# Gram lower triangle on one core: TensorE's loop entered at its last half tile, row turns moved behind the odd tile, one store moved behind the last load

## The chip, the core and the metric

The kernel runs on one core of one Trainium2 chip. The metric is the device time of one execution in microseconds. Everything is float32. TensorE multiplies, VectorE transposes 32x32 blocks, ScalarE copies out of the matmul banks and packs, GpSimd packs what crosses partitions, and SyncE (SP) issues the loads.

## The reference

For each of 2048 batches there is a matrix X of 64 rows and 256 columns. Z = X Xᵀ is 64 x 64, and the output is its strictly lower triangle, row by row, 2016 numbers per batch.

```
Z = jnp.einsum('bnd,bmd->bnm', inputs, inputs)
li, lj = jnp.tril_indices(64, k=-1)
return Z[:, li, lj]
```

134.2 MB are read and 16.5 MB written.

## The kernel before

**Tiles.** A tile is 16 batches, 1 MB of input; there are 128 tiles. SP loads tile t into slot t % 11 of the ring x_in (L193 to L202); from tile 11 on each load waits until tile t-11 has been turned. VectorE turns a tile into x_turned (turn, L242), so that the inner dimension lies on partitions. TensorE multiplies it (multiply, L313): 8 chunks of the inner dimension x 2 slots x 4 quadrants x 2 sides, 128 matmuls in the program, which the profile records as 256 matmuls and 256 weight loads. ScalarE copies the bank set into products (keep, L350).

**The lap.** TensorE's code is a loop over laps of two tiles. The even tile (j = 0) is turned in one transpose of 128x2048 and multiplied behind one wait; the odd tile (j = 1) is turned in two transposes of 128x1024 (chunks 0 to 3 and 4 to 7) and multiplied in two halves, each with its own wait and semaphore. Near the end of each tile TensorE also waits until the other bank set has been copied out. To have one code for all laps, the loop is entered at its second tile (the body "second", L343), so a blank tile of zeros comes first: VectorE and GpSimd fill x_turned[:, 1] with zeros (L278, L222). Its product is never copied out. In memory the code of the body "lap" stands first, then "second".

**Groups.** Eight tiles are a group of 128 batches; there are 16 groups, 0 to 15. When all eight are copied out, VectorE turns the group's rows in 4 pieces of 16 rows (turn_rows, L256), into row_halves; each is one transpose of 128x1024. PIECE_LAG = 10 sets when: behind the turn of tile t, for t = 10, 12, 14 and so on, so behind an even tile, one piece per lap. At t = 126 the remaining pieces of group 14 follow together. ScalarE packs the triangle out of row_halves into packed_rows (pack, L366), in quarters of a piece, two after each tile; GpSimd carries the parts that change partitions (L226 to L232). packed_rows has two buffers, for even and odd groups; before a buffer is written again, ScalarE and GpSimd wait until the stores out of it have landed (wait_packed_free, L149). Group 15 is turned into last_halves, which lies in slots 0 and 1 of x_in, by turn_last_rows (L272).

**Stores.** Groups below LATE_STORES = 13 are stored from ScalarE's queue, after a tile's copy (L393 to L400): even groups in two DMAs of 504 KB, odd groups up to 11 in one of 504, one of 252 and four of 63 KB, spread over the following tiles. The groups from LATE_STORES to 14 are stored by SP behind all its loads (L204 to L207), group 14's other side by ScalarE (L411), and group 15 in three parts by both.

Of the kernel before, what the change touches and what calls it, by code (L numbers as in the profile page):

```python
# [8 lines left out]
HALF = PARTS // 2  # L9
# [10 lines left out]
def gram_lower_triangle(nc: bass.Bass, x: bass.AP, y: bass.AP):  # L20
# [34 lines left out]

    PIECE_LAG = GROUP_TILES + 2
    PACK_LAG = 2 * PIECE_LAG - 2


    BY_POOL = (11, 16)
# [2 lines left out]
                  slice(0, first_column(BLOCK))]  # L65


    FEW, FEW_UNTIL = 4, GROUPS - 4

    LATE_STORES = GROUPS - 3  # L70
    WHOLE_SIDES = [(side, 0, BLOCK) for side in range(SIDES)]
    FIRST_LANES = [(0, 0, BLOCK), (1, 0, BLOCK // 2)]
    FEW_LANES = [(1, q, q + FEW) for q in range(BLOCK // 2, BLOCK, FEW)]
# [4 lines left out]
    with ExitStack() as stack:  # L78
# [3 lines left out]
        def semaphore(name):  # L82
# [14 lines left out]

        last_halves = x_in[:, 0:ROWS * KEPT // (JOINED * DIM)].rearrange(
            "p k (i h j) -> p (k i) h j", h=RUNS, j=BLOCK)

        loaded = [semaphore(f"loaded{k}") for k in range(IN_RING)]

# [41 lines left out]
        def stores_before(group):  # L144

            return sum(16 * len(FIRST_LANES + FEW_LANES if by_few(g) else WHOLE_SIDES)
                       for g in range(group % 2, min(group, GROUPS - 1), 2))

        def wait_packed_free(engine, group):  # L149

            if group >= 2:
                engine.wait_ge(stored[group % 2], stores_before(group))

        def halves(group):
            return last_halves if group == GROUPS - 1 else row_halves

        def pack_short(copy, group, i):
            at = first_column(i)
            return copy(packed_rows[:, group % 2, :, at:at + i], halves(group)[:, i, :, 0:i])  # L159

        def pack_long_pair(copy, group, i):

            at = first_column(i)
            two = packed_rows[:, group % 2, :, at:at + 2 * i].rearrange("p h (w c) -> p h w c", w=2)
            return copy(two[:, :, :, 0:BLOCK], halves(group)[:, i:i + 2].rearrange("p w h j -> p h w j"))  # L165

        def carry_across(copy, group, i, side):

            first, at = side * HALF, first_column(i)
            return copy(packed_rows[first:first + BLOCK, group % 2, :, at + BLOCK:at + i],  # L170
                        halves(group)[first + BLOCK:first + HALF, i, :, 0:i - BLOCK])

        def store(engine, group, columns, lanes):

            rows = y[group * GROUP:(group + 1) * GROUP, columns].rearrange("(h q s) c -> s q h c", h=RUNS, s=SIDES)
            for side, first, end in lanes:
                engine.dma_start(rows[side, first:end],  # L177
                                 packed_rows[side * HALF + first:side * HALF + end, group % 2, :, columns]).then_inc(
                    stored[group % 2], 16)

        def store_last(engine, side, part):
# [58 lines left out]
        @block.vector  # L240
        def _(dve):
            def turn(t):  # L242

                k, (lap, j) = t % IN_RING, place(t)
                dve.wait_ge(loaded[k], (t // IN_RING + 1) * 16)
                for h in range(PARTIALS[j]):
                    chunks = slice(chunks_of(j, h).start, chunks_of(j, h).stop)
                    if laps_done(j, lap) > 0:
                        dve.wait_ge(multiplied[j][h], laps_done(j, lap))  # L249
                    nc.vector.transpose(  # L250
                        x_turned[:, j, chunks].rearrange(
                            "p c b s (h u n v) -> p u v (c b s h) n", h=ROWS // BLOCK, u=PAIRS, v=PAIR),
                        x_in[:, k].rearrange("p (r d) -> p r d", r=JOINED)[
                            :, :, chunks.start * BLOCK:chunks.stop * BLOCK]).then_inc(turned[j][h], LAP)

            def turn_rows(n):  # L256
                group, piece = divmod(n, PIECES)
                rows = piece_rows(piece)
                if piece == 0:

                    wait_kept(dve, (group + 1) * GROUP_TILES - 1)
                if group > 0:

                    dve.wait_ge(packed_home, n - PIECES + 1)
                    if piece < LONG_PIECES:
                        dve.wait_ge(packed_across, (group - 1) * LONG_PIECES + piece + 1)  # L266
                nc.vector.transpose(  # L267
                    row_halves[:, rows].rearrange("p i h (n u v) -> p (i h) u n v", u=PAIRS, v=PAIR),
                    products[:, group % KEPT_RING, rows, :].rearrange("p i (h q) -> p (i h) q", q=BLOCK)).then_inc(
                    rows_turned, 1)  # L270

            def turn_last_rows(run, rows):  # L272

                return nc.vector.transpose(  # L274
                    last_halves[:, rows, run].rearrange("p i (n u v) -> p i u n v", u=PAIRS, v=PAIR),
                    products[:, (GROUPS - 1) % KEPT_RING, rows, run * BLOCK:(run + 1) * BLOCK])

            nc.vector.memset(x_turned[:, 1, 0:CHUNKS // 2], 0.0).then_inc(turned[1][0], LAP)  # L278
            turned_rows = 0
            for t in range(TILES):  # L280
                turn(t)
                if t >= PIECE_LAG and (t - PIECE_LAG) % 2 == 0:
                    turn_rows(turned_rows)
                    turned_rows += 1
                if t == TILES - 2:

                    for n in range(turned_rows, (GROUPS - 1) * PIECES):
                        turn_rows(n)

            for run in range(RUNS - 1):  # L290
                wait_kept(dve, (GROUPS - 1) * GROUP_TILES + (run + 1) * GROUP_TILES // RUNS - 1)
                turn_last_rows(run, slice(0, ROWS))
            wait_last_kept(dve, True)
            turn_last_rows(RUNS - 1, slice(BLOCK, ROWS)).then_inc(rows_turned, LONG_PIECES)
            wait_last_kept(dve, False)
            turn_last_rows(RUNS - 1, slice(0, BLOCK)).then_inc(rows_turned, PIECES - LONG_PIECES)
            wait_packed_free(dve, GROUPS - 1)
            dve.wait_ge(rows_turned, GROUPS * PIECES)  # L298
            for piece in range(LONG_PIECES):
                rows = piece_rows(piece)  # L300
                for i in range(max(BLOCK + 1, rows.start), rows.stop):
                    last = carry_across(nc.vector.tensor_copy, GROUPS - 1, i, 1)
                last.then_inc(last_carried, 1)
            for i in range(1, BY_POOL[0]):
                last = pack_short(nc.vector.tensor_copy, GROUPS - 1, i)
            last.then_inc(last_packed, 1)

        @block.tensor
        def _(pe):

            count = nc.alloc_register(pe.engine, "count")

            def multiply(j):  # L313

                for h in range(PARTIALS[j]):
                    pe.wait_ge(turned[j][h], count)
                    for slot in range(SLOTS):
                        last_slot = h == PARTIALS[j] - 1 and slot == SLOTS - 1
                        if j == LAP - 1 and last_slot:
                            pe.reg_add(count, count, LAP)  # L320
                        for c in chunks_of(j, h):
                            if last_slot and c == CHUNKS - 2:

                                pe.wait_ge(kept[1 - j], count)
                            for g in range(QUADRANTS):
                                for side in range(SIDES):
                                    rows = x_turned[g * BLOCK:(g + 1) * BLOCK, j, c, slot, side]


                                    done = nc.tensor.matmul(  # L330
                                        bank_sets[j][side * HALF:(side + 1) * HALF, g, slot, :].rearrange(
                                            "r (n u v) -> r u n v", u=PAIRS, v=PAIR),
                                        rows,
                                        rows.rearrange("d (h u e) -> d u h e", h=ROWS // BLOCK, u=PAIRS),
                                        start=c == 0 and slot == 0, stop=c == CHUNKS - 1 and slot == SLOTS - 1)

                    done.then_inc(multiplied[j][h], 1)

            pe.reg_mov(count, LAP)
            pe.br("second")  # L340
            with nc.body("lap", valid_engines=[pe.engine]):
                multiply(0)
            with nc.body("second", valid_engines=[pe.engine]):  # L343
                multiply(1)
                pe.br_lt(count, (LAPS + 1) * LAP, on_true="lap", on_false="laps_done")
            nc.switch_bb("laps_done")

# [90 lines left out]
```

## Time and profile before

| | |
|---|---|
| median of 3 runs | 391.2 us (391.16 to 391.91) |
| profiled execution | 390.45 us |
| its span, first to last instruction | 388.6 us |
| TensorE matmul, weight load | 363.6, 358.6 us busy, 33024 records each |
| VectorE | 364.5 us busy, 297 instructions |
| ScalarE | 191.1 us busy, 867 instructions |
| GpSimd | 198.6 us busy, 971 instructions |
| DMA | 150.98 MB, mean 389 GB/s |

The span covers the instructions; the execution's own time has 1.85 us more around it. Busy times do not add up to the span, because the engines work side by side. Matmuls are pipelined, so a busy TensorE is not one at its peak, and one of its instructions may last longer in the profile than the distance to the next. Names in the profile: PE is TensorE, PEld its weight loads, DVE VectorE, ACT ScalarE, POOL GpSimd, SP SyncE; a q behind a name is the engine's sequencer.

### The profile page before, as it was taken

What the parts mean: (1) busy time and instruction counts of PE and PEld (TensorE: products, weight loads), DVE (VectorE), ACT (ScalarE), POOL (GpSimd) and SP (SyncE); (2) the same over time, 40 slices, a digit from 0 to 9 for tenths busy, and PEclk for the clock granted to TensorE, in tenths of its full rate; (3) what the DMA queues carried; (4) which work ended last, traced back from release to release, by engine and by line L of the source; (5) the groups of instructions that cost most, each with busy time, mean ns of one, the idle gap of its engine ahead of it and who ended that gap; (6) DMA issues with size and microseconds to landing.
All of it is one profiled execution on the core that took longest, in us unless ns stands there. A gap on an engine that the chain in (4) does not pass through costs nothing.

```text
span 388.6 us, 68930 instructions
## 1 busy us (share of the span) xinstructions
PE 363.6 (94%) x33024; PEld 358.6 (92%) x33024; DVE 364.5 (94%) x297; ACT 191.1 (49%) x867; POOL 198.6 (51%) x971
## 2 busy tenths in 40 slices
PE   1499999999999999999999999999999999999970
PEld 1499999999999999999999999999999999999970
DVE  3267899999999999999999999999999999999996
ACT  0032246464545555555555555545564545555565
POOL 1000083664828375482827557382846638283766
PEclk9999999999999999999999999999999999999995
DMA  8999999999999999999999999999999999993525
GB/s 309 425 419 422 424 422 417 422 420 423 421 422 420 423 422 421 423 419 422 419 424 418 422 414 425 407 421 422 421 421 370 426 423 422 423 413 141 191 56 164
DMA packets 21433, 150.98 MB, mean 389 GB/s; under 512 B 2720, under 2 KB 2848, under 8 KB 5024
## 3 DMA queue, kind: packets, MB, share of 16 engines
q1 hardware_dynamic: 18912, 136.29, 85.5%
q10 hardware_dynamic: 2496, 14.45, 9.1%
q14 instruction: 21, 0.17, 0.1%
q8 instruction: 4, 0.07, 0.1%
HBM read 134.22 MB, written 16.52 MB: 388 GB/s over the span
## 4 chain that ended last, share of the span: by engine, by line
PE 80%; DMA 7%; DVE 6%; issue 5%; ACT 1%; ACTq 0%; DVEq 0%
PE bank_set L330 80%; DMA x_in<-x_dram 7%; DVE x_turned L250 4%; DVE row_halves L267 1%; DVE packed_rows L170 1%; ACT packed_rows L159 1%; DVE x_in L274 0%; DVE x_turned L278 0%; ACTq L177 0%; ACT products L360 0%; DVEq L249 0%; DVEq L266 0%; ACTq L187 0%; DVEq L298 0%; DVEq L136 0%
## 5 line engine op out<-in xcount | busy, mean ns | idle before, releaser
L330 PE MATMUL bank_set<-x_turned 32*64 32x64 f32 x33024 | 363.6, 235 | 13.6 <-issue 13.3
L330 PEld LDWEIGHTS bank_set<-x_turned 32*64 32x64 f32 x33024 | 358.6, 131 | 18.5 <-issue 13.7
L250 DVE STREAM_TRANSPOSE x_turned<-x_in 128x1024 f32<-128x1024 f32 (+1 forms) x192 | 291.3, 1568 | 19.1 <-PE bank_set L330 13.9
L170 POOL COPY packed_rows<-row_halves 32x32 f32<-32x32 f32 (+30 forms) x930 | 191.6, 206 | 182.7 <-DVE row_halves L267 145.1
L360 ACT COPY products<-bank_set 128x512 f32<-128x512 f32 x129 | 75.1, 583 | 155.0 <-PE bank_set L330 137.0
L267 DVE STREAM_TRANSPOSE row_halves<-products 128x1024 f32<-128x1024 f32 x60 | 72.2, 1205 | 0.0
L159 ACT COPY packed_rows<-row_halves 128x32 f32<-128x32 f32 (+30 forms) x465 | 61.2, 217 | 6.5 <-DVE row_halves L267 6.5
L165 ACT COPY packed_rows<-row_halves 128x128 f32<-128x128 f32 x240 | 54.1, 299 | 9.2 <-DVE row_halves L267 8.8
L360 ACT ACT_TABLE_LOAD x1 | 1.3, 1283 | 21.6 <-PE bank_set L330 21.6
L170 POOL COPY packed_rows<-x_in 32x32 f32<-32x32 f32 (+30 forms) x31 | 5.0, 211 | 2.9 <-DVE x_in L274 2.9
L274 DVE STREAM_TRANSPOSE x_in<-products 128x1024 f32<-128x1024 f32 (+1 forms) x3 | 4.6, 1573 | 0.2 <-ACT products L360 0.2
L165 ACT COPY packed_rows<-x_in 128x128 f32<-128x128 f32 x16 | 3.3, 298 | 1.2 <-DVE x_in L274 1.2
L170 DVE COPY packed_rows<-x_in 32x32 f32<-32x32 f32 (+30 forms) x31 | 3.8, 199 | 0.1
L159 ACT COPY packed_rows<-x_in 128x62 f32<-128x62 f32 (+15 forms) x16 | 2.2, 227 | 0.8 <-DVE packed_rows L170 0.8
L278 DVE MEMSET x_turned<- 128x1024 f32 x1 | 0.9, 912 | 1.0 <-PEq L432 1.0
L222 POOL MEMSET x_turned<- 128x1024 f32 x1 | 1.0, 952 | 0.5 <-POOLq L432 0.5
L159 DVE COPY packed_rows<-x_in 128x2 f32<-128x2 f32 (+9 forms) x10 | 0.9, 171 | 0.0
L159 POOL COPY packed_rows<-x_in 128x22 f32<-128x22 f32 (+4 forms) x5 | 0.9, 222 | 0.1
L432 POOL MEMSET const-float32-0.0<- 128x1 f32 x1 | 0.1, 99 | 0.2 <-issue 0.2
L432 POOL MEMSET const-bfloat16-1.0<- 128x1 bf16 x1 | 0.1, 103 | 0.0
L432 POOL MEMSET const-uint8-127<- 128x1 uint8 x1 | 0.1, 103 | 0.0
L432 POOL MEMSET const-float32-1.0<- 128x1 f32 x1 | 0.1, 99 | 0.0
## 6 DMA issues: line engine op xcount, KB each, us to landing
x_in<-x_dram SPq DMA_DIRECT2D x128, 1024.0 KB, 18.0
y_dram<-packed_rows ACTq DMA_DIRECT2D x21, 504.0 KB, 8.0
y_dram<-packed_rows ACTq DMA_DIRECT2D x6, 252.0 KB
y_dram<-packed_rows ACTq DMA_DIRECT2D x24, 63.0 KB
y_dram<-packed_rows SPq DMA_DIRECT2D x3, 504.0 KB, 4.3
y_dram<-packed_rows SPq DMA_DIRECT2D x1, 222.0 KB
y_dram<-packed_rows ACTq DMA_DIRECT2D x1, 222.0 KB
y_dram<-packed_rows SPq DMA_DIRECT2D x1, 158.0 KB
```

Source lines behind the costliest of these rows:

```text
L159: return copy(packed_rows[:, group % 2, :, at:at + i], halves(group)[:, i, :, 0:i])
L165: return copy(two[:, :, :, 0:BLOCK], halves(group)[:, i:i + 2].rearrange("p w h j -> p h w j"))
L170: return copy(packed_rows[first:first + BLOCK, group % 2, :, at + BLOCK:at + i], halves(group)[first + BLOCK:first + HALF, i, :, 0:i - BLOCK])
L222: nc.gpsimd.memset(x_turned[:, 1, CHUNKS // 2:CHUNKS], 0.0).then_inc(turned[1][1], LAP)
L250: nc.vector.transpose(x_turned[:, j, chunks].rearrange("p c b s (h u n v) -> p u v (c b s h) n", h=ROWS // BLOCK, u=PAIRS, v=PAIR), x_in[: ...
L267: nc.vector.transpose(row_halves[:, rows].rearrange("p i h (n u v) -> p (i h) u n v", u=PAIRS, v=PAIR), products[:, group % KEPT_RING, row ...
L274: return nc.vector.transpose(last_halves[:, rows, run].rearrange("p i (n u v) -> p i u n v", u=PAIRS, v=PAIR), products[:, (GROUPS - 1) % ...
L278: nc.vector.memset(x_turned[:, 1, 0:CHUNKS // 2], 0.0).then_inc(turned[1][0], LAP)
L330: done = nc.tensor.matmul(bank_sets[j][side * HALF:(side + 1) * HALF, g, slot, :].rearrange("r (n u v) -> r u n v", u=PAIRS, v=PAIR), rows ...
L360: nc.scalar.copy(products[:, group % KEPT_RING, rows, in_group * PER_SIDE:(in_group + 1) * PER_SIDE].rearrange("p i (g b) -> p i g b", b=S ...
L432: nc = bacc.Bacc("TRN2", target_bir_lowering=False, num_devices=1)
```

## The change

There are three edits. First, TensorE's loop has three entry places: the body "lap" holds the even tile and the first half of the odd one, the body "last_half" the second half. Before the loop TensorE runs one chunk, 8 matmuls of zeros with start set, which opens the banks of set 1, signals multiplied[1][0], and jumps to "last_half". The zero fill by VectorE covers that chunk's slot alone (128 elements per partition); GpSimd's fill for the second half stays. Second, PIECE_LAG is 9: row pieces are turned behind the odd tiles t = 9, 11 and so on up to 125, and one piece remains for t = 126; PACK_LAG keeps its value, 18. Third, LATE_STORES is 12, so group 12 goes out from SP's queue behind the last load; groups 14 and 15 are packed into late_packed, two buffers in slots 7 to 10 of x_in, and no longer wait for the stores of groups 12 and 13. FEW_UNTIL goes from 12 to 11, which changes no odd group.

```
-    PIECE_LAG = GROUP_TILES + 2
-    PACK_LAG = 2 * PIECE_LAG - 2
+    PIECE_LAG = GROUP_TILES + 1
+    PACK_LAG = 2 * PIECE_LAG
...
-    FEW, FEW_UNTIL = 4, GROUPS - 4
-    LATE_STORES = GROUPS - 3
+    FEW, FEW_UNTIL = 4, GROUPS - 5
+    LATE_STORES = GROUPS - 4
...
+        late_packed = [x_in[:, k:k + 2].rearrange("p k f -> p (k f)")[:, 0:RUNS * PACKED].rearrange(
+            "p (h c) -> p h c", h=RUNS) for k in (TILES % IN_RING, TILES % IN_RING + 2)]
...
+        def packed(group):
+            return packed_rows[:, group % 2] if group < GROUPS - 2 else late_packed[group - (GROUPS - 2)]
...
-            if group >= 2:
+            if 2 <= group < GROUPS - 2:
                 engine.wait_ge(stored[group % 2], stores_before(group))
...
-            nc.vector.memset(x_turned[:, 1, 0:CHUNKS // 2], 0.0).then_inc(turned[1][0], LAP)
+            nc.vector.memset(x_turned[:, 1, 0, 0], 0.0).then_inc(turned[1][0], LAP)
...
-                if t >= PIECE_LAG and (t - PIECE_LAG) % 2 == 0:
+                if PIECE_LAG <= t < TILES - 1 and (t - PIECE_LAG) % 2 == 0:
...
-            def multiply(j):
-                for h in range(PARTIALS[j]):
-                    pe.wait_ge(turned[j][h], count)
+            def multiply_chunk(j, c, slot):
+                for g in range(QUADRANTS):
+                    for side in range(SIDES):
+                        rows = x_turned[g * BLOCK:(g + 1) * BLOCK, j, c, slot, side]
+                        done = nc.tensor.matmul(
...
+                return done
+            def multiply(j, h):
+                pe.wait_ge(turned[j][h], count)
...
             pe.reg_mov(count, LAP)
-            pe.br("second")
+            pe.wait_ge(turned[1][0], LAP)
+            multiply_chunk(1, 0, 0).then_inc(multiplied[1][0], 1)
+            pe.br("last_half")
             with nc.body("lap", valid_engines=[pe.engine]):
-                multiply(0)
-            with nc.body("second", valid_engines=[pe.engine]):
-                multiply(1)
+                multiply(0, 0)
+                multiply(1, 0)
+            with nc.body("last_half", valid_engines=[pe.engine]):
+                multiply(1, 1)
                 pe.br_lt(count, (LAPS + 1) * LAP, on_true="lap", on_false="laps_done")
```

## Rows read from the trace of the kernel before

**Rows 1.** The page: engines' busy time, and GB/s in 40 slices.

```profile
PE 363.6 (94%) x33024; PEld 358.6 (92%) x33024; DVE 364.5 (94%) x297; ACT 191.1 (49%) x867; POOL 198.6 (51%) x971
...
GB/s 309 425 419 422 424 422 417 422 420 423 421 422 420 423 422 421 423 419 422 419 424 418 422 414 425 407 421 422 421 421 370 426 423 422 423 413 141 191 56 164
```

**Rows 2.** The chain in order of time: start us, us, what.

```profile
17.29 302.10 PE bank_set L330 x16507
```

**Rows 3.** Timeline, VectorE near the start: start us, us, what, [idle before].

```profile
32.90 4.57 DVE L250 STREAM_TRANSPOSE x_turned<-x_in 128x2048 f32<-128x2048 f32 x3 [1.03 <-PE bank_set L330]
```

**Rows 4.** Timeline, VectorE from 342 to 350 us.

```profile
342.77 1.21 DVE L267 STREAM_TRANSPOSE row_halves<-products 128x1024 f32<-128x1024 f32 x1
...
343.90 4.54 DVE L250 STREAM_TRANSPOSE x_turned<-x_in 128x1024 f32<-128x1024 f32 x3
...
348.37 1.20 DVE L267 STREAM_TRANSPOSE row_halves<-products 128x1024 f32<-128x1024 f32 x1
```

**Rows 5.** Loads issued in 60:100, then in 250:300 us.

```profile
DMA to landing us min/median/max: 10.7/12.3/13.6
...
DMA to landing us min/median/max: 21.2/23.9/27.3
```

**Rows 6.** Loads of tiles 111, 119 and 127: issue, and to landing.

```profile
L199 SPq DMA_DIRECT2D x_in<-x_dram x1: 328/328/328, 298.1 to 298.1; - x1
...
DMA to landing us min/median/max: 27.3/27.3/27.3
...
L199 SPq DMA_DIRECT2D x_in<-x_dram x1: 327/327/327, 320.5 to 320.5; - x1
...
DMA to landing us min/median/max: 28.8/28.8/28.8
...
L199 SPq DMA_DIRECT2D x_in<-x_dram x1: 328/328/328, 342.9 to 342.9; - x1
```

**Rows 7.** Timeline: row turn and tile 111's turn; tile 119's turn.

```profile
325.99 1.20 DVE L267 STREAM_TRANSPOSE row_halves<-products 128x1024 f32<-128x1024 f32 x1
327.12 1.20 DVE L250 STREAM_TRANSPOSE x_turned<-x_in 128x1024 f32<-128x1024 f32 x1
...
349.49 4.67 DVE L250 STREAM_TRANSPOSE x_turned<-x_in 128x1024 f32<-128x1024 f32 x3
```

**Rows 8.** Timeline of the first 22 us.

```profile
5.04 1.75 PE L330 MATMUL bank_set<-x_turned 32*64 32x64 f32 x94 [5.04 <-issue]
7.08 2.31 DVE L250 STREAM_TRANSPOSE x_turned<-x_in 128x2048 f32<-128x2048 f32 x1 [5.14 <-DMA x_in<-x_dram]
10.71 2.25 PE L330 MATMUL bank_set<-x_turned 32*64 32x64 f32 x128 [3.92 <-issue]
...
18.30 1.25 DVE L250 STREAM_TRANSPOSE x_turned<-x_in 128x1024 f32<-128x1024 f32 x1 [5.40 <-PE bank_set L330]
21.64 1.28 ACT L360 ACT_TABLE_LOAD   x1 [21.64 <-PE bank_set L330]
```

**Rows 9.** DMA queue q8 in 0:20, then whole: packets, MB, share.

```profile
q8 instruction: 3, 0.05, 1.0%
...
q8 instruction: 4, 0.07, 0.1%
```

**Rows 10.** Timeline of the end.

```profile
370.80 2.33 DVE L267 STREAM_TRANSPOSE row_halves<-products 128x1024 f32<-128x1024 f32 x2
...
374.31 2.95 PE L330 MATMUL bank_set<-x_turned 32*64 32x64 f32 x256 [0.34 <-DVE x_turned L250]
...
376.35 0.37 ACTq L177 DMA_DIRECT2D y_dram<-packed_rows  x1
```

**Rows 11.** Group 12's store (issue, to landing); SP's stores from group 13 on.

```profile
L177 ACTq DMA_DIRECT2D y_dram<-packed_rows x2: 327/390/452, 337.7 to 338.0; - x2
...
DMA to landing us min/median/max: 7.2/8.8/10.3
...
358.77 26.98 SPq L177 DMA_DIRECT2D y_dram<-packed_rows  x6
```

More of the change, by code:

```diff
@@ L158, in pack_short @@
             at = first_column(i)
-            return copy(packed_rows[:, group % 2, :, at:at + i], halves(group)[:, i, :, 0:i])
+            return copy(packed(group)[:, :, at:at + i], halves(group)[:, i, :, 0:i])
         def pack_long_pair(copy, group, i):
             at = first_column(i)
-            two = packed_rows[:, group % 2, :, at:at + 2 * i].rearrange("p h (w c) -> p h w c", w=2)
+            two = packed(group)[:, :, at:at + 2 * i].rearrange("p h (w c) -> p h w c", w=2)
             return copy(two[:, :, :, 0:BLOCK], halves(group)[:, i:i + 2].rearrange("p w h j -> p h w j"))
@@ L169, in carry_across @@
             first, at = side * HALF, first_column(i)
-            return copy(packed_rows[first:first + BLOCK, group % 2, :, at + BLOCK:at + i],
+            return copy(packed(group)[first:first + BLOCK, :, at + BLOCK:at + i],
                         halves(group)[first + BLOCK:first + HALF, i, :, 0:i - BLOCK])
@@ L177, in store @@
                 engine.dma_start(rows[side, first:end],
-                                 packed_rows[side * HALF + first:side * HALF + end, group % 2, :, columns]).then_inc(
+                                 packed(group)[side * HALF + first:side * HALF + end, :, columns]).then_inc(
                     stored[group % 2], 16)
@@ L311, in _ @@
             count = nc.alloc_register(pe.engine, "count")
-            def multiply(j):
-                for h in range(PARTIALS[j]):
-                    pe.wait_ge(turned[j][h], count)
[L317 to L337, printed above, removed]
@@ new lines, in multiply_chunk @@
+            def multiply_chunk(j, c, slot):
[3 more added lines that the diff above has]
+                        done = nc.tensor.matmul(
+                            bank_sets[j][side * HALF:(side + 1) * HALF, g, slot, :].rearrange(
+                                "r (n u v) -> r u n v", u=PAIRS, v=PAIR),
+                            rows,
+                            rows.rearrange("d (h u e) -> d u h e", h=ROWS // BLOCK, u=PAIRS),
+                            start=c == 0 and slot == 0, stop=c == CHUNKS - 1 and slot == SLOTS - 1)
+                return done
@@ new lines, in multiply @@
+            def multiply(j, h):
+                pe.wait_ge(turned[j][h], count)
+                for slot in range(SLOTS):
+                    last_slot = h == PARTIALS[j] - 1 and slot == SLOTS - 1
+                    if j == LAP - 1 and last_slot:
+                        pe.reg_add(count, count, LAP)
+                    for c in chunks_of(j, h):
+                        if last_slot and c == CHUNKS - 2:
+                            pe.wait_ge(kept[1 - j], count)
+                        done = multiply_chunk(j, c, slot)
+                done.then_inc(multiplied[j][h], 1)
```

## The prediction

> **What bounds the kernel now.** I read the page's busy shares first, then the chain of waits, the timelines of start and end, and the landing times of loads. TensorE and VectorE are each busy for 94% and DMA moves some 421 GB/s up to the last five slices [rows 1], so the page alone does not say which of them a saving must reach. The chain has one unbroken TensorE piece from 17.29 to 319.39 us [rows 2]. There are three regimes.
>
> The lap of two tiles: with no finished rows to turn, VectorE is busy for 4.57 us and waits 1.03 for TensorE [rows 3]: TensorE's lap is 5.60. Later VectorE's lap is a row turn at 342.77, two half turns and a full one from 343.90, and the next row turn at 348.37: also 5.60, with no idle time [rows 4]. Both are full; neither can catch up.
>
> The loads: tile t's load goes out when tile t-11 is turned, some 30 us ahead of its use. It takes a median 12.3 us to land in 60:100 and 23.9 in 250:300 [rows 5]: DMA is full, and every store pushes the loads later. Near the end the margin is nearly gone. Tile 111 lands at 298.1 + 27.3 = 325.4 and is turned at 327.12: 1.7 early. Tile 119: 320.5 + 28.8 = 349.3 against 349.49: 0.2 [rows 6, 7]. A TensorE further ahead than these margins waits for loads.
>
> The entry: TensorE starts at 5.04, idles 3.92 before 10.71, and 4.33 before 17.29 [rows 2, 8], in "issue", so for no semaphore.
>
> **Entering at the last half.** Before, a whole blank tile runs: 94 + 128 matmul records, then 34 behind 17.29 (256 a tile, two per matmul of the program, each with a weight load). The instruction queue q8 fetches three times in 0:20 and once later, 0.07 MB in four [rows 9], 16 KB a time. Between two stops stand 128 matmuls with 128 weight loads, 256 instructions. So I read a stop as the first visit to a block of 256 instructions, at 3.9 to 4.3 us.
>
> The new layout follows. The body "second" began with 94 pairs (189 instructions) left in the third block, at about 578; some 514 of those ahead are tile 0's code, 64 the preamble. The chunk of 8 matmuls adds 16 pairs, 32 instructions. The body "last_half" then starts at about 867: 78 of its 128 pairs lie in block four, 50 in block five. Block three is first reached inside tile 0, after some 208 of its 256 pairs. Three stops again, one now in real work.
>
> Step by step: the chunk takes 16 x 19 ns (1.75 / 94, [rows 8]) = 0.3, and I put 0.3 for its wait for the zero fill (estimate), so the last half starts 0.6 later, at 5.6. 78 x 19 ns = 1.5: 7.1. A stop, 4.1: 11.2. 50 pairs, 0.9: 12.1. Tile 0 is turned by 7.08 + 2.31 = 9.4, and took from 18.2 (VectorE was released at 18.30) to 21.64, 3.4 us [rows 8]; 208 of 256 pairs are 2.8: 14.9. A stop, 4.3: 19.2. The rest 0.6: 19.8. Lead 1.8 us. Bounds: if block three comes ahead of need, 12.1 + 3.4 = 15.5, a lead of 6.1; if one more stop is paid, 1.8 - 4.3 = -2.5. I take 1.8, because in the trace every new block is waited for.
>
> The Trainium skill (Runtime: NRT & Kernel Launch, section Instruction fetch mechanics) says that instructions come in 16 KiB blocks of 256, prefetched sequentially, and that a taken branch out of a two-page window forces a fetch. Its block size agrees with the 128 pairs between the stops. Its two-page window would stop every lap at the jump back; the trace disagrees: unbroken from 17.29 on. Its hidden sequential prefetch would make the lead 6.1; the stops of 3.92 and 4.33 speak against that.
>
> **Row turns behind the odd tile.** The count stays 60; only VectorE's order changes: from full, row turn, half, half to full, half, half, row turn. A lap's sum stays 5.60, and the rows it needs were copied off the banks a tile earlier. The price: an odd tile is turned where the row turn stood, 1.13 us sooner (343.90 - 342.77, [rows 4]), and its load must land that much sooner. Tile 111's margin falls from 1.7 to 0.6 (325.99 against 325.4), tile 119's from 0.2 to -0.9 [rows 6, 7]. Alone, this edit loses the 0.9 and gains the 0.5 below: +0.4. ScalarE and GpSimd get the rows sooner; both have idle time, 49% and 51% busy [rows 1], so that is worth nothing.
>
> At the end it gains. Before, VectorE turned two row pieces between tiles 126 and 127 (370.80, 2.33 us), so TensorE waited 0.34 for tile 127 at 374.31 and took 2.95 for it, to 377.26 [rows 10]. Now one of the two stands ahead of tile 126, and VectorE is ready 1.1 sooner. TensorE flows from 373.97 at half a lap per tile, 2.80: 376.77, a gain of 0.5. ScalarE must be free to copy: its half store at 376.35 takes 0.37 [rows 10], just in time, and what it packs before that comes sooner as well. Each us that it is late would come off this gain. Bounds 0 to 0.5; I take 0.5.
>
> **Group 12's store behind the last load.** Its two issues leave ScalarE's queue at 337.7 [rows 11] for SP's, behind tile 127's load at 342.9 [rows 6]. 2 x 504 KB are 1.03 MB, at 421 GB/s 2.45 us of all DMA engines. Loads from tile 118 or 119 on land up to 2.45 sooner: tile 119 at 346.9, wanted at 348.37. Margin 1.5 there, where it would have been -0.9. Bounds: 0 if the late DMA engines are late for another reason, 2.45 as taken. The tail pays nothing: the last load lands by 342.9 + 28.8 - 2.45 = 369.3, group 12's store behind it by 371.7, group 13's (issued at 358.77, [rows 11]) by 374.2, ahead of group 14's halves at 376.35, and DMA moves only 56 to 191 GB/s from about 350 on [rows 1]. ScalarE's two issues (0.33 to 0.45 each, [rows 11]) fall into idle time.
>
> The late buffers in x_in take away waits that would bite now: group 14's last piece is turned at 370.80 [rows 10], its first three laps sooner, at 354; held for a store that lands at 371.7, ScalarE would be over 10 us late. With the buffers nobody waits for it.
>
> The Trainium skill (DMA: Bandwidth & Descriptors, section Queues, rings and completion order) says that a queue's descriptors are consumed in ring order on each DMA engine, while the engine takes turns between queues. The trace agrees: ScalarE's store landed after 7.2 to 10.3 us, a load took 28.8 [rows 6, 11]. By that rule a store in SP's own queue cannot delay a load.
>
> **The sum**, against the profiled execution (390.45 us: span 388.6 and 1.85 around it). The lead of 1.8 lasts until the loads bind. The tightest place is then tile 111: 0.6, less 0.1 from landing to start, leaves 0.5 from there on. With the end's 0.5 that is 1.0: 389.45. The median of the runs, 391.2, lies 0.75 above the profiled execution; if that is lateness of loads, it moves the old bound (tile 119) and the new one (tile 111) alike, so I take the same 1.0 off: 390.2 us.
>
> **Rivals.**
> 1. The loads do not bind at tile 111: the whole 1.8 is kept, 1.8 + 0.5 = 2.3: 388.9. For: the margin is a small difference of large numbers, and 1.3 us earlier landing is enough. Against: the loads fall behind steadily [rows 5].
> 2. Nothing to measure. Either the end's gain alone is left (tile 111 lands 0.5 later, or the entry is not earlier at all, since a stop stays in tile 0): 390.7. Or the store's move relieves the wrong DMA engines and the odd tiles' earlier turns meet late loads: 391.6. For: tile 119's margin of 0.2. Against: 2.45 us of traffic fewer in exactly that stretch.
> 3. Slower: the entry skips three blocks where it skipped one, and one more of them is missing at the jump back into the loop. Tile 0 then ends 2.5 us later than before; TensorE is unbroken behind it, so 2.5 - 0.5 = +2.0: 393.2. It decides if four stops of 4 us stand ahead of tile 0's end; my count is three. Against: before, the first two blocks were there at that jump, without a stop.
>
> **How the numbers follow.** Forecast 0.50 (own range 389.6 to 390.4), rival 1 0.12, rival 2 0.28, rival 3 0.10. The measurement can tell 0.2%, 0.8 us, from no change. Faster 0.62, within it 0.28, slower 0.10. Range 388.7 to 391.8: all but rival 3.
>
> **What would show it.** TensorE: 16 matmul records before 2.5 us, three stops, one of them inside tile 0, whose end is at 19 to 20 us. A lead of 1.8 us at 100 us, of 0.5 at 340. VectorE idle for a load at tile 111 or near it. The last tile's matmuls directly behind tile 126's. Time to landing under 27 us from tile 119 on. It is wrong if tile 0 ends after 21.6, if loads bind at tiles 119 to 121 again, or if the end is more than the 11.3 us of before (388.6 - 377.26) behind the last matmul.

## The result: 14.5 us slower, and the loss stands in the first 45 us

The changed kernel takes 405.55 us (405.2 to 406.27, 6 runs), the kernel before 391.01 in the same comparison: ratio 1.0374, 95% interval 1.0358 to 1.039. I had forecast 390.2. In the profiled execution the span is 403.8 us against 388.6, 15.2 more.

The page of the kernel after answers to [rows 1]: TensorE is as busy in us as before, but in a longer span, and the loss is at its left end.

```profile
PE 366.2 (91%) x32912; PEld 360.8 (89%) x32912; DVE 364.4 (90%) x297; ACT 186.1 (46%) x867; POOL 197.1 (49%) x971
...
PE   2425999999999999999999999999999999999980
...
PEclk9955999999999999999999999999999999999996
...
GB/s 323 423 418 302 287 373 371 362 358 426 419 422 400 403 427 416 419 393 426 422 420 409 411 425 419 419 377 425 412 425 393 421 422 422 424 369 219 157 26 179
```

Four slices pass before TensorE is full (before, two). DMA falls to 287 GB/s in the fifth, because the load ring is full and is emptied late (the loads of tiles 13 and 14 go out at 28.3 and 39.5): the loads are ahead now. The timeline of the kernel after answers to [rows 8]. Its columns: start us, us, what, and in brackets the idle time ahead.

```profile
1.05 0.52 PE L329 MATMUL bank_set<-x_turned 32*64 32x64 f32 x16 [1.05 <-DVE x_turned L287]
...
6.45 1.54 PE L329 MATMUL bank_set<-x_turned 32*64 32x64 f32 x78 [4.88 <-issue]
...
13.12 4.41 PE L329 MATMUL bank_set<-x_turned 32*64 32x64 f32 x256 [5.12 <-issue]
...
24.76 2.26 PE L329 MATMUL bank_set<-x_turned 32*64 32x64 f32 x128 [7.24 <-issue]
25.93 1.28 ACT L377 ACT_TABLE_LOAD   x1 [25.93 <-PE bank_set L329]
...
30.96 2.26 PE L329 MATMUL bank_set<-x_turned 32*64 32x64 f32 x128 [3.94 <-issue]
...
36.99 23.25 PE L329 MATMUL bank_set<-x_turned 32*64 32x64 f32 x1987 [3.77 <-issue]
...
44.71 0.58 ACT L377 COPY products<-bank_set 128x512 f32<-128x512 f32 x1 [2.14 <-PE bank_set L329]
```

The counts of pairs (a weight load and its matmul) come first: 16, 78, then 256, which is the blank half's last 50 pairs and tile 0's first 206. Up to there it is the forecast. Then a stop of 7.24 and, 128 pairs apart, two more that I had not foreseen. ScalarE's first instruction is released by the end of tile 0's product, at 25.93 (before, 21.64). The last row is the copy of tile 3; before it stood at 29.97. The delay there, 14.74 us, is nearly that of the whole run, since every engine runs in step behind it: the copy of tile 125 is 15.6 us late, that of tile 127 15.06.

DMA queue q8, which fetches code, answers to [rows 9]: 0:20, 20:50, and the whole run.

```profile
q8 instruction: 3, 0.05, 0.9%
...
q8 instruction: 4, 0.07, 0.9%
...
q8 instruction: 7, 0.11, 0.1%
```

Seven fetches where there were four. The trace has each fetch as one packet of q8, of 16 KB, so the DMA view in narrow windows places them. Times are us from the span's start.

| packet of q8 | TensorE, changed kernel |
|---|---|
| 4.00 to 4.88 | resumes at 6.45, block four |
| 10.65 to 11.63 | resumes at 13.12, block five |
| 16.80 to 17.83 | no stop ends; block three is reached at 17.53 |
| 22.39 to 23.46 | resumes at 24.76, block three |
| 28.51 to 29.61 | resumes at 30.96, block four |
| 34.51 to 35.61 | resumes at 36.99, block five |
| 38.13 to 39.08 | no stop ends |

In all runs of this document TensorE resumes 1.2 to 1.6 us behind the end of a packet, at every stop in "issue" (in the kernel before the packets end at 3.63, 9.24 and 15.91, and TensorE resumes at 5.04, 10.71 and 17.29). So the stops are waits for code. Which block a packet holds the trace does not say; the table gives the block that TensorE enters.

The wait of the first jump itself is a row too, of TensorE's sequencer: 4072 ns before (first fence), 5272 after (second).

```profile
L340 PEldq COMPARE_BRANCH  x1: 4072/4072/4072, 0.9 to 0.9; - x1
```

```profile
L356 PEldq COMPARE_BRANCH  x1: 5272/5272/5272, 1.1 to 1.1; - x1
```

Loads of tiles 111 and 119 (answer to [rows 6], and their turns to [rows 7]): 313.6 + 20.7 = 334.3, turned at 341.53, 7.2 us early; 336.0 + 22.2 = 358.2, turned at 363.95, 5.7 early. Nothing waits for a load late in this run.

```profile
L207 SPq DMA_DIRECT2D x_in<-x_dram x1: 328/328/328, 313.6 to 313.6; - x1
...
DMA to landing us min/median/max: 20.7/20.7/20.7
...
L207 SPq DMA_DIRECT2D x_in<-x_dram x1: 328/328/328, 336.0 to 336.0; - x1
...
DMA to landing us min/median/max: 22.2/22.2/22.2
...
341.53 1.20 DVE L258 STREAM_TRANSPOSE x_turned<-x_in 128x1024 f32<-128x1024 f32 x1
...
363.95 1.20 DVE L258 STREAM_TRANSPOSE x_turned<-x_in 128x1024 f32<-128x1024 f32 x1
```

The end answers to [rows 10]: one row turn ahead of tile 127 in place of two, and TensorE has no wait for VectorE in its last piece; ScalarE's half store ends 0.1 us ahead of the last copy (before, 0.6).

```profile
386.37 1.21 DVE L275 STREAM_TRANSPOSE row_halves<-products 128x1024 f32<-128x1024 f32 x1
387.50 2.33 DVE L258 STREAM_TRANSPOSE x_turned<-x_in 128x1024 f32<-128x1024 f32 x2
...
391.89 0.38 ACTq L185 DMA_DIRECT2D y_dram<-x_in  x1
392.36 0.65 ACT L377 COPY products<-bank_set 128x256 f32<-128x256 f32 x2 [0.50 <-PE bank_set L329]
```

### The profile page after: what moved, and what is told of

It reads as the page before. It is cut to its first block, busy times and chain, and to the rows that moved or that the text cites. A ratio compares the mean times of both kernels' runs of the same rounds, so it can differ in the third digit from the quotient of the medians.

```text
span 403.8 us, 68701 instructions
## 1 busy us (share of the span) xinstructions
PE 366.2 (91%) x32912; PEld 360.8 (89%) x32912; DVE 364.4 (90%) x297; ACT 186.1 (46%) x867; POOL 197.1 (49%) x971
## 4 chain that ended last, share of the span: by engine, by line
DVE 39%; PE 36%; issue 23%; ACT 1%; POOL 0%; DVEq 0%; ACTq 0%; POOLq 0%
PE bank_set L329 36%; DVE x_turned L258 29%; DVE row_halves L275 10%; DVE x_in L178 1%; ACT x_in L167 1%; DVE x_in L282 0%; POOL x_turned L230 0%; DVEq L274 0%; ACTq L185 0%; ACT products L377 0%; DVEq L257 0%; ACTq L195 0%; POOLq L227 0%; DVEq L140 0%; POOLq L229 0%
## 5 line engine op out<-in xcount | busy, mean ns | idle before, releaser
L178 POOL COPY packed_rows<-row_halves 32x32 f32<-32x32 f32 (+30 forms) x868 | 177.4, 204 | 186.5 <-DVE row_halves L275 151.4
L167 ACT COPY packed_rows<-row_halves 128x32 f32<-128x32 f32 (+30 forms) x434 | 57.2, 219 | 0.0
L173 ACT COPY packed_rows<-row_halves 128x128 f32<-128x128 f32 x224 | 50.5, 301 | 4.9 <-issue 4.9
L178 POOL COPY x_in<-row_halves 32x32 f32<-32x32 f32 (+30 forms) x62 | 12.7, 204 | 9.7 <-DVE row_halves L275 7.2
L178 POOL COPY x_in<-x_in 32x32 f32<-32x32 f32 (+30 forms) x31 | 4.9, 210 | 5.9 <-DVE x_in L282 5.9
L167 ACT COPY x_in<-row_halves 128x32 f32<-128x32 f32 (+30 forms) x31 | 3.9, 218 | 0.0
L173 ACT COPY x_in<-x_in 128x128 f32<-128x128 f32 x16 | 3.3, 295 | 1.1 <-DVE x_in L282 1.1
L178 DVE COPY x_in<-x_in 32x32 f32<-32x32 f32 (+30 forms) x31 | 3.7, 199 | 0.0
L173 ACT COPY x_in<-row_halves 128x128 f32<-128x128 f32 x16 | 3.6, 303 | 0.0
```

The source lines that it names most:

```text
L167: return copy(packed(group)[:, :, at:at + i], halves(group)[:, i, :, 0:i])
L178: return copy(packed(group)[first:first + BLOCK, :, at + BLOCK:at + i], halves(group)[first + BLOCK:first + HALF, i, :, 0:i - BLOCK])
```

## The experiments

**Which edit it is.** The kernel before with the new entry alone:

```
-            pe.br("second")
+            pe.wait_ge(turned[1][0], LAP)
+            multiply_chunk(1, 0, 0).then_inc(multiplied[1][0], 1)
+            pe.br("last_half")
```

> The kernel before with the new entry alone (chunk, jump to last_half, small zero fill). Theory J (jump over blocks of code): the jump skips block three, so that block and then the two behind it are fetched again inside tiles 0 and 1: five stops as in the changed kernel, 7 fetches on q8, tile 3 copied 14.7 us later than before, and since nothing catches up, the whole time is 14.5 to 15.5 us over before (405.5 to 406.5). Rival R (the row turn order or the moved store costs the time): within 1 us of before, 390 to 392.

Measured: 406.38 us, ratio 1.0396 (1.0372 to 1.0419), 7 fetches, and the same sequence on TensorE with a first long stop of 8.74:

```profile
12.91 4.00 PE L320 MATMUL bank_set<-x_turned 32*64 32x64 f32 x256 [4.58 <-issue]
25.66 2.25 PE L320 MATMUL bank_set<-x_turned 32*64 32x64 f32 x128 [8.74 <-issue]
31.86 2.25 PE L320 MATMUL bank_set<-x_turned 32*64 32x64 f32 x128 [3.95 <-issue]
37.90 7.33 PE L320 MATMUL bank_set<-x_turned 32*64 32x64 f32 x508 [3.79 <-issue]
```

The entry is the whole loss. Tile 3 is copied 15.9 us later than before, where I had expected 14.7; the first jump (5612 ns) and the long stop are longer than in the changed kernel. Its complement, the changed kernel with the old entry:

```
-            multiply_chunk(1, 0, 0).then_inc(multiplied[1][0], 1)
-            pe.br("last_half")
+            pe.br("second")
```

> The changed kernel with the old entry (jump to the second body, whole blank tile), so row turns behind the odd tile and group 12 behind the last load alone. Theory J: 0.5 us less at the last tile, as the changed kernel's trace shows (15.6 us late at tile 125, 15.06 at tile 127), and up to 0.9 us more from a lap that is 0.01 us longer: ratio 0.998 to 1.001, 390.2 to 391.4. Rival R: 400 to 406.

Measured: 390.29 against 391.01, ratio 0.9981 (0.9971 to 0.9991): 0.7 us faster. The other two edits one by one, first PIECE_LAG = GROUP_TILES + 1 alone:

> The kernel before with PIECE_LAG 9 alone: row turns behind the odd tile. By my forecast's terms: 0.5 us gained at the last tile, 0.9 lost where tile 119's load lands late: +0.4, 391.4; VectorE idle for a load near 349 us. If the longer lap of the changed kernel (0.01 us, 64 laps) comes from this order, up to 0.7 more. If loads do not bind: -0.5, 390.5.

Measured: 390.58 us, ratio 0.9996 (0.9984 to 1.0007), no change to be seen. In its trace tile 119's load lands 0.7 us ahead of its turn and no turn behind tile 0's waits for a load, so the forecast loss of 0.9 did not come; the copies drift 0.6 us later against the kernel before between tiles 3 and 118 (a lap of 5.60 in place of 5.59), and the last two tiles win 0.55 back. Then the store and the late buffers alone (FEW_UNTIL goes along):

```
-    LATE_STORES = GROUPS - 3
+    LATE_STORES = GROUPS - 4
```

> The kernel before with the store of group 12 behind the last load and the late buffers alone. By my forecast's terms tile 119's load lands 2.45 us sooner relative to its turn, and TensorE gains only the 0.1 us that it lost there: 390.8 to 391.1. If the loads of before bind more than its profiled execution shows (the median is 0.75 over it), up to 0.8 less: 390.2.

Measured: 390.42 us, ratio 0.9986 (0.9975 to 0.9996), 0.6 us faster. In its profile the smallest margin of a load behind tile 1 is 2.4 us (tile 114), where it was 0.1 (tile 120). That more is gained than the 0.1 us of the profiled execution would fit loads that bind in the kernel's common run, which is 0.75 us longer than the profiled one; no profile of such a run exists, so this is not shown.

**Is it the skipped block?** First the chunk with a jump to the first block not yet fetched, block three, where the odd tile's first half lies. The chunk is closed by itself (alone sets its stop) and signals nothing; the zero fill is the large one again.

```
-            multiply_chunk(1, 0, 0).then_inc(multiplied[1][0], 1)
-            pe.br("last_half")
+            multiply_chunk(1, 0, 0, alone=True)
+            pe.br("odd")
             with nc.body("lap", valid_engines=[pe.engine]):
                 multiply(0, 0)
+            with nc.body("odd", valid_engines=[pe.engine]):
                 multiply(1, 0)
-            with nc.body("last_half", valid_engines=[pe.engine]):
                 multiply(1, 1)
```

> The changed kernel with its chunk of 8 matmuls (opened and closed by itself), but the jump behind it goes to the first half of the odd tile, so to the next block of code (block three), and the whole blank odd tile runs. Theory J (the jump over a block is the cause): three stops as in the kernel before, at 79, 128 and 49 pairs (32 instructions of chunk shift the borders by 16 pairs), 4 fetches on q8, tile 3 some 1 to 2.5 us later than before for the later first jump, 391.5 to 393.5. Rival K (the chunk or the split of the loop's code costs it, wherever the jump goes): 404 to 407.

Measured: 394.49 us, 1.0088 (1.0064 to 1.0112). Three stops, ahead of 78, of 128 and of the rest, and 4 fetches:

```profile
1.99 0.52 PE L329 MATMUL bank_set<-x_turned 32*64 32x64 f32 x16 [1.99 <-DVE x_turned L287]
9.16 1.55 PE L329 MATMUL bank_set<-x_turned 32*64 32x64 f32 x78 [6.65 <-issue]
14.72 2.25 PE L329 MATMUL bank_set<-x_turned 32*64 32x64 f32 x128 [4.02 <-issue]
21.32 30.91 PE L329 MATMUL bank_set<-x_turned 32*64 32x64 f32 x2707 [4.35 <-issue]
```

So the chunk and the split bodies are innocent. The time is 1 us over my range: the jump stands behind the fill and the chunk and waits 7032 ns (resumed at 9.16, before at 5.04). Second, five more chunks ahead of the jump, to move every border:

```
+            for _ in range(5):
+                multiply_chunk(1, 0, 0, alone=True)
             multiply_chunk(1, 0, 0).then_inc(multiplied[1][0], 1)
```

> The changed kernel with six chunks ahead of the jump in place of one, 160 instructions more, so last_half begins at about 1027, the start of block five. Theory J: all borders move by 80 pairs: one stop at the entry, 128 pairs of the blank half and 128 of tile 0 without a stop, then a long stop (7 to 9 us) for block three, and block four and five fetched after it with a stop of 3.8 to 4 each, 128 pairs apart; one fetch fewer on q8 (6), and some 4 us less than the changed kernel: 401 to 402.5. If the stops go with the jump and not with blocks of 256 instructions, the pairs between them stay 78, 256, 128, 128 and the time 405 to 408.

Measured: 407.80 us, 1.0427 (1.0391 to 1.0463), 7 fetches where I had expected 6. I had missed a border by two pairs:

```profile
1.05 1.78 PE L329 MATMUL bank_set<-x_turned 32*64 32x64 f32 x96 [1.05 <-DVE x_turned L287]
8.98 2.25 PE L329 MATMUL bank_set<-x_turned 32*64 32x64 f32 x126 [6.15 <-issue]
14.35 2.66 PE L329 MATMUL bank_set<-x_turned 32*64 32x64 f32 x128 [3.12 <-issue]
21.37 2.26 PE L329 MATMUL bank_set<-x_turned 32*64 32x64 f32 x128 [4.36 <-issue]
27.85 2.26 PE L329 MATMUL bank_set<-x_turned 32*64 32x64 f32 x128 [4.22 <-issue]
34.05 2.25 PE L329 MATMUL bank_set<-x_turned 32*64 32x64 f32 x128 [3.94 <-issue]
39.52 12.70 PE L329 MATMUL bank_set<-x_turned 32*64 32x64 f32 x974 [3.22 <-issue]
```

The blank half no longer fits block five: 126 pairs, a stop, 2 pairs in block six; then 126 pairs of tile 0, and blocks three to six one after another, 128 pairs each. The borders moved with the instructions, as blocks of 256 must; six blocks are in play, so the time rose where I forecast a fall. The time alone would fit the rival (405 to 408); the counts of pairs do not.

The very long stop is gone here, 4.36. The packets of q8 fit a fetch of block six that stood in the way in the changed kernel. There the packet from 16.80 to 17.83 ends no stop, TensorE reaches block three at 17.53, and the next packet ends 5.6 us behind it: 7.24 is the rest of one fetch, a whole one, and the 1.3 us up to the next matmul. Here TensorE leaves block six after 2 pairs, and no packet lies between the one that ends at 13.04, for block six, and the one that ends at 19.87, behind which block three starts.

Third, the same entry with an empty stub in block three that holds only a jump:

> The changed kernel, entered at the same last half in the same place in memory, but by way of block three: the jump behind the chunk goes to a stub between tile 0's code and the odd tile's first half (at about 612, block three), which holds only a jump to last_half (block four); tile 0's code jumps over the stub in each lap. Theory J (skipping block three is the cause): block three is there when tile 0 needs it, so blocks four and five are not fetched again: 4 or 5 fetches on q8 in place of 7, 256 pairs of tile 0 in one piece, tile 3 copied 9 to 13 us sooner than in the changed kernel, 392 to 396. Rival K2 (entering with block four as the first fetched one, or jumping back from it over two blocks, is the cause): 7 fetches, 404 to 407.

Measured: 406.16 us, 1.0388, 7 fetches. It tested nothing: the stub held no other instruction, and the program laid out has no jump of its line, nor one over it. So the opening chunk itself was put into block three:

```
-            multiply_chunk(1, 0, 0).then_inc(multiplied[1][0], 1)
-            pe.br("last_half")
+            pe.br("opening")
             with nc.body("lap", valid_engines=[pe.engine]):
                 multiply(0, 0)
+                pe.br("first_half")
+            with nc.body("opening", valid_engines=[pe.engine]):
+                multiply_chunk(1, 0, 0).then_inc(multiplied[1][0], 1)
+                pe.br("last_half")
+            with nc.body("first_half", valid_engines=[pe.engine]):
                 multiply(1, 0)
```

> The changed kernel with the opening chunk itself placed in block three, between tile 0's code and the odd tile's first half, followed by the jump to last_half in block four. The entry jumps to the chunk; tile 0's code jumps over it in each lap (k_stub's stub held no instruction and was laid out away, so it tested nothing). Theory J (block three was skipped, so the blocks behind it were fetched twice): the first jump waits 4.1 us as in the kernel before, then 16 pairs, 78, 50; tile 0 runs in one piece; 4 fetches on q8; tile 3 copied within 1 us of the kernel before's 29.97, whole time 390 to 392.5. Rival K2 (the last half as entry, whatever was visited ahead of it, is the cause): 7 fetches and 404 to 407.

Measured: 399.58 us, 1.0226 (1.0207 to 1.0246). The start is nearly as forecast: four fetches and tile 0 in one piece behind the third stop. The first jump waits 4964 ns, not 4.1 us, and tile 3 is copied at 31.37, so 1.4 us later than before (I had said within 1) and 13.3 sooner than in the changed kernel.

```profile
6.06 0.52 PE L329 MATMUL bank_set<-x_turned 32*64 32x64 f32 x16 [6.06 <-issue]
11.93 1.53 PE L329 MATMUL bank_set<-x_turned 32*64 32x64 f32 x77 [5.35 <-issue]
17.56 32.67 PE L329 MATMUL bank_set<-x_turned 32*64 32x64 f32 x2758 [4.10 <-issue]
...
80.13 0.58 ACT L381 COPY products<-bank_set 128x512 f32<-128x512 f32 x1 [1.51 <-PE bank_set L329]
...
194.76 0.59 ACT L381 COPY products<-bank_set 128x512 f32<-128x512 f32 x1 [1.51 <-PE bank_set L329]
...
L358 PEldq COMPARE_BRANCH  x64: 163/163/176, 22.2 to 383.6; - x64
```

Same entry point, block three visited ahead of it, and no block is fetched twice: the skip is the cause. But the whole time is 7 us over my range. The copies of tiles 20 and 60 are 114.63 us apart, 5.73 a lap: the jump over the opening takes 163 ns each time, and here nearly all of it is paid: 0.14 us.

**An order with no skip.** The last half placed first in memory, right behind the chunk; the lap then has a jump more.

```
+            with nc.body("last_half", valid_engines=[pe.engine]):
+                multiply(1, 1)
+                pe.br_lt(count, (LAPS + 1) * LAP, on_true="lap", on_false="laps_done")
             with nc.body("lap", valid_engines=[pe.engine]):
                 multiply(0, 0)
                 multiply(1, 0)
-            with nc.body("last_half", valid_engines=[pe.engine]):
-                multiply(1, 1)
-                pe.br_lt(count, (LAPS + 1) * LAP, on_true="lap", on_false="laps_done")
+                pe.br("last_half")
```

> The changed kernel with last_half placed first in memory, right behind the chunk, and an unconditional jump at the end of the lap's first part: nothing is skipped at the entry, but each lap has a second jump. Theory J: no block is fetched twice, 4 fetches on q8 or fewer; the blank half runs at once; blocks three, four and five are met in tiles 0 and 1 at 79, 128 and 128 pairs. If each is fetched only when it is reached, three stops of 4 us in real work, tile 1 ends near 28.6 (before 24.3). If the next block is fetched while TensorE waits for tile 0's load, one or two stops are gone and tile 1 ends at 20 to 25. The second jump costs 0 to 0.1 us in each of 64 laps. Together 390 to 401. Rival K (entering at the last half is bad wherever it lies): 404 or more.

Measured: 389.93 against 391.16, ratio 0.9963 (0.9948 to 0.9978), at the very low end of my 390 to 401.

```profile
1.97 2.26 PE L329 MATMUL bank_set<-x_turned 32*64 32x64 f32 x128 [0.40 <-POOL x_turned L230]
...
7.97 3.49 PE L329 MATMUL bank_set<-x_turned 32*64 32x64 f32 x206 [3.73 <-DVE x_turned L258]
...
15.27 2.27 PE L329 MATMUL bank_set<-x_turned 32*64 32x64 f32 x128 [3.81 <-issue]
...
21.47 30.78 PE L329 MATMUL bank_set<-x_turned 32*64 32x64 f32 x2683 [3.93 <-issue]
```

Entering at the last half is not bad in itself. Tile 0 crosses into block three after some 79 pairs, within the 206 of that row, without a stop: q8's first packet ends at 7.65, while TensorE waited 3.73 us for tile 0. Blocks four and five begin 6.2 us apart (15.27, 21.47), of which 2.3 are work. The extra jump costs nothing that the lap shows here: of the lap's two jumps one takes 76 ns and one 169, together 245, where the one before took 208; and the lap is 5.59.

**What sets the 6 us?** f_last_half_first with fewer loads outstanding at the start:

```
             def load(t):
                 k = t % IN_RING
+                if 2 <= t < 8:
+                    sync.wait_ge(loaded[(t - 2) % IN_RING], 16)
```

> f_last_half_first, and SP issues the loads of tiles 2 to 7 only when the load two tiles ahead of each has landed, so no more than two loads are outstanding up to some 20 us. Theory Q (a block of code costs 6.2 us from one to the next, because its fetch of 16 KB queues behind outstanding loads): the fetches follow each other in 4 to 5 us, the stops of 3.8 and 3.9 fall to 1.5 to 2.5, tile 1 is copied at 20 to 22 us in place of 24.67. Of this lead the loads let 1.5 us through (the smallest margin of f_last_half_first, 1.58 us at tile 111), so 388 to 389. Rival F (the time of a fetch is fixed): the same stops, and the same time as f_last_half_first, 389.9, or later if the loads fall behind.

Measured: 390.80 us, ratio 0.9994 (0.9979 to 1.0008); I had expected 388 to 389 if outstanding loads delay the fetches, and 389.9 or later if they do not. The first stop fell to 1.16 us, the second did not, and tile 1 was copied at 21.68, 3 us sooner. Then loads bound: two of VectorE's four waits for loads are those of tiles 0 and 1, the others those of tiles 103 and 111; tiles 103, 111 and 113 were turned the moment they had landed, and the lead was all but gone by tile 110.

```profile
12.51 1.62 PE L331 MATMUL bank_set<-x_turned 32*64 32x64 f32 x128 [1.16 <-issue]
18.43 13.77 PE L331 MATMUL bank_set<-x_turned 32*64 32x64 f32 x1074 [4.31 <-issue]
...
DVE x_turned L260 <- DMA x_in<-x_dram: 8.0, 4, 4.6
```

With three outstanding (3 <= t < 8, waiting for t - 3):

> The same with three loads outstanding. Theory Q: between f_last_half_first and g_f_pace2 at the stops (2.5 to 3.5 us), and DMA never idle, 388.3 to 389.5. Rival F: 389.9.

Measured: 389.39 against 391.22, ratio 0.9949 (0.9935 to 0.9963), the fastest of all here, 1.8 us under the kernel before and 16.2 under the changed one. Its stops are 3.35 and 3.94, and tile 1 is copied 0.24 us sooner than in f_last_half_first; the 0.5 us between these two kernels' times is not clear of noise, since their intervals overlap. The pacing of two on the kernel before:

> The kernel before with the same pacing as g_f_pace2 alone. Theory Q: stops of 1.5 to 2.5 us in place of 3.92 and 4.33, tile 1 copied 3 to 4 us sooner; but tile 119's margin of 0.2 us is used up at once, so the whole time gains 0 to 0.3 us: 390.7 to 391.2. Rival F: as before, or later by what the loads lose.

Measured: 393.61 us, 1.0057 (1.0039 to 1.0076), 2.4 us slower, where I had expected a gain of up to 0.3. Its stops are 3.10 and 4.06 and its start is 0.5 us earlier, but DMA moved 365 GB/s in 10:20, and with no margin behind it the run loses 3.5 us of that lead between tiles 100 and 120. Outstanding loads explain a part of some stops, not the 6 us. Where the fetches follow each other, the packets of q8 end 5.5 to 6.8 us apart with ten loads outstanding and with three. With two they are 3.6, 5.9 and 5.1 apart in g_f_pace2, 4.8 and 6.2 in j_before_pace2. What else makes the 6 us stays open.

Last, both ideas: i_f_pace3 with the opening chunk in block three, in the middle of tile 0's code, so one jump more in each lap than there, two more than in the kernel before.

> i_f_pace3 (last half first in memory, three loads outstanding at the start) with the opening chunk in block three, in the middle of tile 0's code, and the entry by way of it. Entering a block starts the fetch of the next, 6 us each, whatever runs there: block three is there at 5.0 (the wait of the first jump as in the kernel before, 4.1), four near 11, five near 17, in place of 9, 15 and 21. Blank half and tile 0 run on resident code from 5.4 to 11; one stop of about 4 us ahead of block five; tile 1 copied at 20 to 21 us, 3.5 us sooner than i_f_pace3. The loads let 2.3 us of it through (its smallest margin, 2.36): 387 to 388. Rival: entering block three starts nothing while the code jumps back, and block four is fetched only when it is reached: 389.4 as i_f_pace3.

Measured: 394.32 us, 1.0093 (1.0079 to 1.0106), 6.3 us over my range.

```profile
6.00 2.62 PE L331 MATMUL bank_set<-x_turned 32*64 32x64 f32 x144 [6.00 <-issue]
9.49 5.06 PE L331 MATMUL bank_set<-x_turned 32*64 32x64 f32 x332 [0.87 <-DVE x_turned L260]
18.38 31.84 PE L331 MATMUL bank_set<-x_turned 32*64 32x64 f32 x2696 [3.83 <-issue]
...
76.41 0.59 ACT L387 COPY products<-bank_set 128x512 f32<-128x512 f32 x1 [1.48 <-PE bank_set L331]
...
190.35 0.59 ACT L387 COPY products<-bank_set 128x512 f32<-128x512 f32 x1 [1.49 <-PE bank_set L331]
```

The start does nearly what was forecast: 16 pairs in block three, back for the blank half, and then 332 pairs across two borders with one stop behind them; tile 1 is copied at 21.63, 2.8 us sooner than in i_f_pace3 (forecast: 3.5). The packet behind the visit to block three ends at 10.46, and TensorE then runs through block four without a stop: the visit of 16 pairs had started the fetch of the next block, though TensorE left at once. That is not so at every visit: in h_after_pad160 the packet behind the 2 pairs in block six is block three's. But the lap is 5.70 (113.94 us for 20), and 0.1 us in each of 64 laps eats the start twice over.

## Why the prediction was wrong

**Entry: the failed step.** "Three stops again, one now in real work" was right for the three that it named (after 16, 94 and 350 pairs) and wrong in what stands behind: I took a block once fetched to stay. The runs show that after a jump over an unfetched block, that block and every block behind it are fetched when the code comes back to it in sequence (7 packets where there were 4): a stop of 7.24 us in place of the forecast 4.3 ahead of block three, and two more, of 3.94 and 3.77, ahead of blocks four and five. Tile 0 ends at 25.93, past the 21.6 that I had named as the sign of being wrong. The sum: the unbroken run starts at 36.99 in place of 17.29, 19.7 later. By then TensorE has done 462 pairs of real work (606 less 144 blank), and before it still owed 34 blank ones; these 496 pairs are 5.4 us at 5.60 / 512 ns each. 19.7 - 5.4 = 14.3, against 14.74 at tile 3; the last 0.4 I cannot place. Rival 3 came nearest: a skip of blocks that makes one of them missing at the jump back, one stop more ahead of tile 0's end, +2.0. Its mechanism was there, its size was not: as many stops stand ahead of tile 0's end as forecast, the last 2.9 us longer, and two more stand in tile 1. Its chance of 0.10 was too small for a step of which the trace of before could show nothing, since that kernel never skips.

The rule of the Trainium skill that I weighed here comes out mixed. The page Runtime: NRT & Kernel Launch (section Instruction fetch mechanics) says that the next block is prefetched in sequence and that a taken branch breaks this. I had held the stops of 3.92 and 4.33 against the first half; f_last_half_first and m_f_open_in_block3 show the prefetch, at some 6 us a block. It is hidden only where TensorE comes to the next block that much later, because it waits or runs other code meanwhile. The second half is in line with what the changed kernel paid for, though the page does not speak of fetching blocks again. Its two-page window stays refuted: no lap stops at its jump back.

**The first jump.** Forecast to resume at 5.6, it did at 6.45: the jump waits 5272 ns in place of 4072, not only 0.2 us later. The later it is issued, the longer it waited in nearly all runs here: issued at 0.9, it took 4.1 to 4.4 us; at 1.0, 4.9 to 5.0; at 1.1, 5.3 to 6.1; at 2.1, 7.0; at 2.4, 6.6.

**Row turns.** The order cost no wait for a load: in the trace of c_order_only tile 119's landed 0.7 us early where I had put it 0.9 late. A lap longer by 0.01 us, which I had put at zero, took 0.6; why it is longer stays open. The end's gain, forecast 0.5, was 0.55 in c_order_only; in the changed kernel the copies are 15.62 us late at tile 125 and 15.06 at tile 127, 0.56.

**Store.** In d_store_only tile 119's load landed 4.5 us ahead of its turn, where it was 0.2: more than the 2.45 that I had put, of which 0.4 is that run's later start. The edit alone was worth 0.6 us; my terms give 0.1.

**The sum of the rest.** Without the entry my terms give -0.5, the end's gain; b_rest_only measured -0.7. The binding loads at tile 111 that capped my lead never came into play in the changed kernel. In g_f_pace2 and j_before_pace2 loads did bind, with waits for those of tiles 102 to 118, but there fewer loads had been outstanding at the start.

## What to carry to other kernels

A jump in a loop's first pass is a matter of code layout. If it passes over code that has not been fetched, that code and the blocks behind it are fetched on the way back, at some 6 us a block here, and a kernel that runs in step for the rest of its time carries that to the end. So enter a loop where its code begins, or in the first block that is not yet there, and change the order of the bodies in memory rather than jump further forward. Count the price of a jump by the laps: 0.1 us in 64 laps outweighed a start that was 3 us better.

## What the runs showed that was not expected

- Consecutive blocks of 256 instructions began 5.4 to 7.0 us apart in h_after_pad160 (8.98, 14.35, 21.37, 27.85, 34.05, 39.52), whatever ran in them; only with two loads outstanding did one come within 3.5 (block four at 12.51 in g_f_pace2, entered from block three, which TensorE had reached at about 9).
- On its first visit a block runs slowly: 128 pairs took 2.25 us, 17.6 ns each, where the lap has 10.9. The granted clock was 1.00 for most of these stretches (0:20 us), and about 0.52, mostly the lower of its two levels (1.2 GHz), in 20:40 of the changed kernel, where TensorE had stood idle for 7.24 us and worked 7.5 of 20; 128 pairs took 2.26 there too. So it is not the clock alone; behind the stop of only 1.16 us in g_f_pace2 the same 128 pairs took 1.62, in a stretch (10:20) whose granted clock was 0.72. What it is stays open.
- Jumps of the same form took 73 to 76 ns or 163 to 213. Laps with 208 and 245 ns of jumps ran in 5.59 us, those with 376 in 5.73 and those with 399 in 5.70.
